# Five static instruction lists of a four-layer gated transformer kernel: new priority numbers, and a planner that sees two more dependences

## The reference

```python
x = x + tanh(g_xattn[0]) * linear_attention(ctx, norm(x))   # 16 heads of 16, features exp(z), exp(-z)
x = x + tanh(g_ffn[0])   * butterfly_ffn(norm(x))           # 256 -> 1024, 10 butterfly stages, gelu, 10 stages, -> 256
x = x + tanh(g_xattn[1]) * softmax_attention(norm(x), ctx, mask)
x = x + tanh(g_ffn[1])   * lora_moe(norm(x))                # top 2 of 8 experts, rank 4, beside a dense 256x256
x = x + tanh(g_xattn[2]) * softmax_attention(norm(x), ctx)
x = x + tanh(g_ffn[2])   * bitlinear_ffn(norm(x))           # ternary weights, 8-bit activations, 256 -> 1024 -> 256
x = x + tanh(g_xattn[3]) * softmax_attention(norm(x), ctx, mask)
x = x + tanh(g_ffn[3])   * gated_lora_ffn(norm(x))          # top 2 of 8 experts, silu(h1) * h3, 256 -> 1024 -> 256
```

## Time and profile before

| what | value |
|---|---|
| median of three runs | 2890.6 us |
| the profiled execution | 2893.2 us |
| its span, first to last instruction | 2891.2 us |
| mean granted TensorE clock | 0.984 |
| PE, DVE, ACT, POOL busy | 91%, 60%, 40%, 32% |
| filler products (L820) | 543, 137.9 us |

### The profile page before, as it was taken

How to read it: one execution, slowest core, us unless ns; L and a number is a source line. 1 busy time by engine, 2 the same in 40 slices (tenths; PEclk the granted TensorE clock), 3 DMA queues, 4 the chain that set the end, 5 groups by cost and what they waited for, 6 DMA issues and landing times.

```text
span 2891.2 us, 55150 instructions
## 1 busy us (share of the span) xinstructions
PE 2621.1 (91%) x21811; PEld 1739.4 (60%) x21811; DVE 1724.6 (60%) x4702; ACT 1142.6 (40%) x1853; POOL 939.1 (32%) x2408
## 2 busy tenths in 40 slices
PE   4889988899999998899999998889999999889999
PEld 3447654576676654466667664447667665446666
DVE  6753588855534568866434457985543456886532
ACT  4644535522234444542233543542323453553211
POOL 1022232243334323233333333233333332323333
PEclk8999999999999999999999999999999999999999
DMA  4020000000000000000000000000000000000000
GB/s 168 1 87 11 11 2 13 1 1 8 8 12 15 11 1 1 13 1 8 8 8 14 5 11 1 11 1 1 9 8 18 9 11 1 1 1 1 5 4 8
DMA packets 18733, 37.00 MB, mean 13 GB/s; under 512 B 3600, under 2 KB 13872, under 8 KB 17456
## 3 DMA queue, kind: packets, MB, share of 16 engines
q1 hardware_dynamic: 18480, 33.48, 3.3%
HBM read 29.28 MB, written 4.19 MB: 12 GB/s over the span
## 4 chain that ended last, share of the span: by engine, by line
PE 65%; DVE 22%; issue 4%; ACT 4%; POOL 4%; SPq 1%; DMA 0%; DVEq 0%; POOLq 0%; ACTq 0%
PE P L1244 7%; PE P L1103 4%; PE P L1128 4%; PE P L1277 4%; PE P L1115 4%; PE P L1056 4%; PE P L1064 4%; DVE mx L1661 3%; PE P L1253 3%; PE P L1245 3%; PE P L1262 3%; PE P L1036 3%; PE P L957 3%; PE P L926 2%; PE P L833 2%
## 5 line engine op out<-in xcount | busy, mean ns | idle before, releaser
L1661 DVE TENSOR_REDUCE mx<-P 128x8 f32<-128x1232 f32 x256 | 367.9, 1437 | 239.6 <-PE P L962 83.9
L1244 PE MATMUL P<-xT,w 128*128 128x256 f32 x1024 | 269.8, 386 | 6.3 <-DVE xT L1703 5.1
L732 POOL TENSOR_TENSOR sm<-sm 128x2 f32<-128x2 f32 x384 | 77.0, 200 | 582.3 <-DVE sm L1657 561.9
L1712 DVE SCALAR_TENSOR_TENSOR x<-P,w_gates,x 128x512 f32<-128x512 f32 x112 | 83.9, 749 | 295.4 <-PE P L1278 123.5
L1417 ACT ACTIVATE ET<-P 128x2048 f32<-128x2048 f32 x96 | 180.1, 1876 | 193.6 <-PE P L1039 111.6
L1244 PEld LDWEIGHTS P<-xT,w 128*128 128x128 f32 x1024 | 192.9, 192 | 66.6 <-issue 19.0
L1370 ACT ACTIVATE xn<-x,sm 128x256 f32<-128x256 f32 x256 | 139.5, 592 | 207.7 <-POOL sm L740 207.2
L957 PE MATMUL P<-KB,R 32*128 32x308 f32 x1536 | 158.0, 469 | 49.2 <-ACT ET L1417 35.1
L1468 ACT ACTIVATE gu<-P 128x256 f32<-128x256 f32 x128 | 49.0, 383 | 372.6 <-PE P L1245 332.3
L1036 PE MATMUL P<-R,KB 32*128 32x256 f32 x2048 | 165.1, 409 | 9.3 <-DVE mx L1661 9.2
L785 POOL TENSOR_TENSOR xn<-xn,gu 128x512 f32<-128x512 f32 x64 | 81.1, 1268 | 256.4 <-DVE xn L1881 256.4
(11 more groups left out here) (302 smaller groups left out, 5797.8 us busy)
## 6 DMA issues: line engine op xcount, KB each, us to landing
kvw<-in_wkv SPq DMA_DIRECT2D x12, 672.0 KB, 4.0
x<-in_x SPq DMA_DIRECT2D x16, 256.0 KB, 2.8
out<-x SPq DMA_DIRECT2D x16, 256.0 KB, 2.1
w<-in_w SPq DMA_DIRECT2D x2, 1024.0 KB, 8.5
w<-in_wexp SPq DMA_DIRECT2D x1, 1028.0 KB, 7.3
w_w<-in_wcon SPq DMA_DIRECT2D x1, 1024.0 KB, 9.3
R<-in_m3t SPq DMA_DIRECT2D x1, 1024.0 KB, 10.9
R<-in_w1q SPq DMA_DIRECT2D x1, 1024.0 KB, 12.8
```

Of the source, the lines that this page charges most:

```text
L1244: e.matmul(o, wm[:, c, js], s.xT[:, c, :], start=n == c == 0, stop=False, skip_group_check=True)
L1661: e.tensor_reduce(s.mx[:, i, :, 2 * u:2 * u + 2], quad[:, :, 0:2 * NK].rearrange("p g (a k) -> p g a k", a=2), AX.X, ALU.max).then_inc(q_d, 1)
```

## The change

It leaves every stage's instructions and waits as they are and changes the planner: two dependences more in `late` and `early`, another table BACK (more stages have a number), and two terms more in the rank of a part: 18 ns for each attention that its stream has finished, and 5 ns for the stream's index. The instructions themselves are the same, but for the number of fillers.

```diff
--- before.py
+++ after.py
@@ -320,6 +320,10 @@
 
             if engine == "DVE" and name == "h1" and of[2] > 1:
                 return [("back", of[2] - 2)]
+            if name == "near" and engine == "PE":
+                return [("mat", *of)]
+            if name == "mat" and engine == "ACT" and of[1] >= 4:
+                return [("near", of[0], of[1] - 4)]
             if engine == "ACT" and name in ("h1", "h2"):
                 n = half(name, of[2]) - 2
                 return [("half", n)] if n >= 0 else []
@@ -334,6 +338,8 @@
 
             if name == "back":
                 return "back", of[1]
+            if (name, engine) in (("mat", "DVE"), ("near", "PE")):
+                return name, *of
             if engine == "DVE" and name in ("h1", "h2"):
                 return "half", half(name, of[2])
             return ("bias",) if name == "bias" else None
@@ -483,16 +489,21 @@
                 yield "store", s, b
 
 
-        BACK = {"PE": {"down": -293, "down_there": 961, "exa": -486, "gate1": 1037, "h2": -790, "mw": -45, "near":
-                -167, "pv": 210, "pz": -1740, "tl": -5, "tsum": -130, "up": 22, "upt": 95, "w2": -29},
-                "ACT": {"ex": 8, "gate1": -826, "gate3": -2072, "gelu2": -186, "h1": -119, "h2": -255, "key": -846,
-                "mat": -968, "mt": 62, "near": 299, "norm": -121, "pv": -172, "q1": 86, "q2": 97, "qp": -56, "sts":
-                600, "turn": 43, "up": 234, "val": 223, "wide": -1626},
-                "DVE": {"down": 54, "e3": -216, "exa": -3100, "f3": -1123, "gate1": 432, "gate3": 79, "gelu2": 2064,
-                "h1": -107, "lin": 550, "no": 301, "norm": -138, "out": 40, "tern": 601, "top1": 370, "top3": 1054,
-                "upt": -1191, "val": -210, "w1": -44, "wide": 283},
-                "POOL": {"bias": 499, "down_there": 442, "hw": 144, "no": -167, "norm": -313},
-                "SP": {"kvw": -987, "late": -1105, "masks": -51, "store": 1715}}
+        BACK = {"PE": {"back": -342, "down": -259, "down_there": 1204, "exa": -241, "f3": -149, "gate1": 2018,
+                "gate3": 43, "h1": 2, "h2": -84, "key": -247, "lin": 410, "mw": -1294, "near": -137, "out": -27,
+                "pv": 200, "pz": -2271, "q1": 234, "q2": -126, "qp": -41, "sc": 1, "st": -1, "sts": 242, "tl": -37,
+                "tsum": -129, "turn": -18, "up": 14, "upt": -2332, "val": -35, "w1": -7, "w2": 2},
+                "ACT": {"down_there": -2096, "ex": -1396, "gate1": 532, "gate3": 410, "gelu2": 616, "h1": 317,
+                "key": 807, "mat": -111, "mt": -626, "mw": -876, "near": -40, "norm": -100, "pv": 250, "q1": -216,
+                "q2": 932, "qp": -392, "st": 224, "sts": -3751, "tl": -1946, "turn": -353, "up": -719, "val": -2024,
+                "wide": -578},
+                "DVE": {"down": 751, "e3": -373, "exa": -1984, "f3": 132, "gate1": -48, "gate3": -2896, "gelu2":
+                4000, "h1": -604, "h2": -3545, "lin": 861, "masks": 391, "mat": 159, "mx": 110, "near": 108, "no":
+                956, "norm": -2156, "out": 833, "q1": 742, "q2": -3292, "split": -2568, "tern": 255, "top1": 709,
+                "top3": 1237, "tsum": 1256, "val": -3144, "w1": 65, "w2": -470, "wide": 278},
+                "POOL": {"bias": 203, "down_there": -360, "hw": -1041, "key": 348, "mw": 1109, "no": 1370, "norm":
+                201},
+                "SP": {"kvw": 492, "late": 4, "masks": -1183, "store": 1080}}
 
         def orders():
 
@@ -574,7 +585,7 @@
                                 can.append((i, p))
                 if not can:
                     break
-                i, p = min(can, key=lambda c: (start(c[1]) + BACK[c[1][2]].get(c[1][1], 0),
+                i, p = min(can, key=lambda c: (start(c[1]) + BACK[c[1][2]].get(c[1][1], 0) + 18.0 * count[c[0]] + 5.0 * c[0],
                                                count[c[0]] + 0.3 * c[0]))
                 at = start(p)
                 if p[2] == "ACT":
```

## The result

The changed kernel takes 2826.2 us (median; 2817.1 to 2830.5), the kernel before 2892.5 in the same comparison: ratio 0.9767, 95% interval 0.9739 to 0.9794. 2870.6 us with a range down to 2838 had been forecast: the direction was right, the size was not.

What follows compares the result with a forecast made beforehand. PE, busy 91% of the span, was taken as the bound; -4 (masks stall), -8 (folding chain) and -8 (new numbers) gave -20 us, so 2870.6 us as median. Range 2838 to 2899, the forecast's own 2855 to 2884.8.

Steps and rivals of the forecast that it cites:

- Bound: Whole kernel: PE is the bound, so time can come only from its idle time, fillers and running at the lower clock.
- 81.4 us called scattered: PE idle time left after the start, folding, DVE-heavy stretches and end, scattered over the other 1,695 us.
- Part 1: First 205 us: the two new dependences stop the planner placing folding products before their matrix is made; -4 and -8 us.
- (a): Before about 32 us: DVE stands for the masks' DMA and PE waits 7.54 us; -4 us, between 0 and -7.5.
- (b): Folding chain from 46.8 us: 23.0 us idle ahead of its products, a third goes; -8 us, between -23 and +10.
- The clock: After the early stall PE ran at a lower clock; removing the stall might return 3.3 us more, left out of the sum.
- Part 2: PE's waits: new holding-back numbers shorten some and lengthen others, a tenth each; net -8 us, between -35 and +20.
- The rows that I had named as taken earlier: PE's waits for ET (ex), mt, split and xn, together 91.6 us; a tenth was to go, -9.2 us.
- The rank terms: 18 ns per finished attention and 5 ns per stream index only settle near ties; priced at nothing.
- 3: DVE-heavy stretches: the new order shifts streams against each other and levels DVE; -45 us, 2846 us, chance 0.18.
- 1: Folding ends earlier, but the gain is given back in the DVE-heavy stretch from 400 to 600 us; 2889 us, chance 0.13.
- 2: Second half of DVE-heavy stretches: holding DVE's gelu2 and the normaliser costs +15.5 us; 2906 us, chance 0.22 with others slower.

Runs made afterwards that it cites:

- e1: The kernel before plus the two dependences alone, old numbers and rank kept: 2947.5 us, ratio 1.0206 to the kernel before.
- e2: The changed kernel without the two dependences, new numbers and rank terms kept: 2823.2 us, ratio 0.9774 to the kernel before.
- e5: The changed kernel with the masks moved behind the matrix, copies and first wide stage in DVE's list: 2826.4 us, ratio 0.9762 to the kernel before.
- e13: The changed kernel with fillers in gaps from 0.4 us, folding included (536), and the masks later in DVE's list: 2820.4 us, ratio 0.9737 to the kernel before.
- e14: The changed kernel with fillers also in the folding stretch's gaps from 0.4 us (456 instead of 404): 2830.0 us, ratio 0.9771 to the kernel before.
- e3: The kernel before with new numbers and rank terms only for parts planned from 200 us on, no new dependences: 2835.7 us, ratio 0.9807.
- e6: The changed kernel with every number of BACK moved randomly by up to 30 ns: 2979.6 us, ratio 1.0284 to the kernel before.
- e11: The kernel before with every number of its BACK moved randomly by up to 30 ns: 2956.2 us, ratio 1.0215.
- e7: The changed kernel without the two rank terms (18 and 5 ns): 2910.8 us, ratio 1.0054 to the kernel before.
- e4: The kernel before with new numbers and rank terms only for parts planned before 200 us, no new dependences: 2882.9 us, ratio 0.9965.
- e8: The changed kernel with all 404 fillers taken out of PE's list: 2835.5 us, ratio 0.9798 to the kernel before.

## Why the prediction was wrong

The forecast was -20 us, measured were -66. By its own steps:

- *Bound.* Right: PE's idle time and fillers are what can go, and 73.8 of their 408.0 us went. But the fillers, of which 35.0 us went, got no term, and neither did the stretch at the end of each batch, which lost 9.9 us a batch and lay mostly in the 81.4 us called scattered.
- *Part 1, that the two dependences bring the folding's gain.* Wrong, by e1 and e2. The size came out near by luck, for another reason: the new numbers gave 10.9 us up to the first store, 12 had been forecast.
- *(a), -4 for the stall.* It stayed (7.68 us), and when e5 and e13 remove it no gain shows.
- *(b), -8.* The idle time it named fell by 12.1 us, from 23.0 to 10.9; but not by the dependences, the main reason given: in e2, without them, the folding products wait 20.2 + 1.8 + 1.9 = 23.9 us in all, against the changed kernel's 24.4.
- *The clock, 3.3 us left out.* e14 lifts the clock over the first 205 us from 0.92 to 0.98 and e5, without the stall, over 17.1 to 205 us from 0.91 to 0.94, and neither has a time that is clear of the changed kernel's. So leaving it out did no harm.
- *Part 2, -8 for the numbers.* This is the step that failed. It was -52 to -57: 51.8 us come after the first store in the traces, and e3, with the new numbers from 200 us on alone, is 57 us faster than the kernel before. I weighed each number against the row of the wait that it seemed to act on and took a tenth of it. The rows that I had named as taken earlier fell by 17.5 us, from 91.6 to 74.1, two tenths instead of one; but xn and mt fell by 26.5 and `split`'s grew by 11.4, against its sign, as POOL's `no` fell against its own. And the greater part lay outside these rows: 35.0 us of fillers and waits that I hadn't named. e6 and e11 show that such a weighing can't be repaired by better shares: with the same numbers to 30 ns the time is 153 us higher. The lower end, -35, was again a share of those rows; the 201 us lost in the four DVE-heavy stretches and 81 us in each batch were the true stock to bound it by. That all low ends together give 2825, next to the time measured, is chance: it has (a)'s -7.5, which didn't come, and (b)'s -23, where 12.1 us of idle time went.
- *The rank terms, priced at nothing.* Wrong by 85 us (e7). "Small against a gap" is no measure where a near tie decides and everything behind it follows.
- *That a changed rule of the planner can do harm* was never priced: e1 shows a cost of 2% for a truer model with the old table. No rival had it.
- *Rivals.* 3 came nearest in time (2846, chance 0.18), but its mechanism isn't what is seen: DVE is still at 90% in its heavy stretch, not levelled. Some of it is there: 7 us more of PE's needed work lie beside DVE's heavy part in a batch. 1 fails on e3 and e4, 2 on the waits for POOL's `no` and on the time.

What stays open: which of the many near ties, and which engine's numbers, make the better list. None of the runs isolates one tie, one stage or one engine, and the windows say only where the lost time went down. Open too is why the start's 10 us reach the end in e4, and the 3 to 5 us of e5 and e14 don't.

## What to carry to other kernels

A table of priorities for a greedy planner acts as a whole, not as a sum of effects: don't predict it number by number, but ask how much lost time (idle and filler) there is over the whole span, and take the planner's own count of gaps as the sign of which way it went: here the order of the twelve kernels with one rule for fillers is the same by fillers and by ratio, though not the size (111 more than before cost 0.5% in e7, 147 more 2.1% in e1). Where that rule itself changes the sign fails: e8 has the least lost time and isn't the fastest. Don't change the planner's rules and keep the table without measuring. A stall that is easy to see in a trace can be worth little or nothing: move one entry of the list by hand and measure before pricing it.

## What had not been expected

Leaving out 404 products that nobody reads, 102.9 us of PE's time, made the kernel 9 us slower, and with 132 more, 80 of them in short gaps of the batches, it was 8 us faster (by intervals that overlap slightly). And two lists whose planner's numbers differ by 30 ns at most differ by 5.3% in time (2826.2 and 2979.6 us).
